# Two 1024-wide scans per unit, the carried state added by GpSimd, and a C product shared differently between VectorE and GpSimd

## The reference

```python
def step(h, inputs):
    u_t, dt_t, B_t, C_t = inputs
    dA = jnp.exp(dt_t[:, :, None] * A[None])
    dBu = (dt_t * u_t)[:, :, None] * B_t[:, None, :]
    h = dA * h + dBu
    y = jnp.einsum('bdn,bn->bd', h, C_t)
    return (h, y)
...
A = -jnp.exp(A_log)
y = _selective_scan(u_c, dt, A, Bm, Cm, D)
y = y * jax.nn.silu(z)
out = jnp.einsum('ble,de->bld', y, W_out)
return x + out
```

## Time and profile before

| | |
|---|---|
| time, median of 3 runs | 2322.84 us (2321.6 to 2324.49) |
| time of the profiled execution | 2327.84 us |
| its span, first to last instruction | 2325.9 us |
| busy: TensorE / VectorE / ScalarE / GpSimd | 77% / 81% / 78% / 83% |
| mean granted clock of TensorE | 0.888 of full speed |

### The profile page before, as it was taken

How to read it: one execution, slowest core, us unless ns; L and a number is a source line. 1 busy time by engine, 2 the same in 40 slices (tenths; PEclk the granted TensorE clock), 3 DMA queues, 4 the chain that set the end, 5 groups by cost and what they waited for, 6 DMA issues and landing times.

```text
span 2325.9 us, 32531 instructions
## 1 busy us (share of the span) xinstructions
PE 1795.3 (77%) x7694; PEld 923.0 (40%) x7694; DVE 1893.7 (81%) x2437; ACT 1806.5 (78%) x3753; POOL 1933.7 (83%) x1190
## 2 busy tenths in 40 slices
PE   5566768697878788797878788797878788666785
PEld 2112323153534344353434444353434344343542
DVE  0389988899889888899889888899889888999221
ACT  5888888888898788888998788888998787763332
POOL 1588897989999898999999898999999898987333
PEclk9888978797989898998989898997989898786998
DMA  1635454477777786677777786677777786797332
GB/s 57 145 83 141 105 141 109 125 177 184 169 178 178 169 213 160 170 183 184 174 175 180 163 218 157 171 183 180 176 179 178 160 221 147 183 259 221 70 49 34
DMA packets 217979, 369.34 MB, mean 159 GB/s; under 512 B 31040, under 2 KB 86592, under 8 KB 217664
## 3 DMA queue, kind: packets, MB, share of 16 engines
q1 hardware_dynamic: 192208, 333.56, 58.1%
q0 software_dynamic: 25584, 33.71, 7.5%
HBM read 285.05 MB, written 83.01 MB: 158 GB/s over the span
## 4 chain that ended last, share of the span: by engine, by line
issue 23%; POOL 23%; ACT 18%; PE 18%; DVE 9%; DMA 8%; POOLq 0%; ACTq 0%; DVEq 0%; SPq 0%
DMA out<-yt,xt 8%; POOL arena L1324 8%; DVE dA L1116 5%; PE ring L603 5%; ACT dA L979 4%; POOL arena L1332 4%; POOL out L1372 3%; POOL sorted_x L1362 2%; PE yps L697 2%; PE ring L611 2%; DVE arena L1116 2%; POOL arena L1347 2%; POOL arena L1342 1%; PE p_g L729 1%; PE ring L640 1%
## 5 line engine op out<-in xcount | busy, mean ns | idle before, releaser
L1324 POOL TENSOR_TENSOR arena<-arena,b_bc 128x2048 f32<-128x2048 f32 x256 | 998.4, 3900 | 88.3 <-PE yps L697 88.3
L979 ACT ACTIVATE dA<-arena,a_s 128x512 f32<-128x512 f32 x1024 | 680.5, 684 | 116.0 <-DVE arena L1125 69.9
L1116 DVE TENSOR_TENSOR_SCAN dA<-dA,arena 128x512 f32<-128x512 f32 x384 | 454.5, 1213 | 156.8 <-ACT dA L979 107.3
L1116 DVE TENSOR_TENSOR_SCAN dA<-dA,carry,arena 128x512 f32<-128x512 f32 x384 | 477.6, 1274 | 52.3 <-POOL arena L1324 36.2
L697 PE MATMUL yps<-arena,const_s 128*32 128x512 f32 x2048 | 320.4, 702 | 59.9 <-POOL arena L1332 35.9
L1332 POOL TENSOR_TENSOR arena<-arena,c_bc 128x511 f32<-128x511 f32 (+1 forms) x256 | 335.0, 1308 | 28.3 <-DVE arena L1116 26.5
L1125 DVE TENSOR_TENSOR arena<-dA,c_bc 128x1024 f32<-128x1024 f32 x256 | 313.6, 1225 | 8.8
L1372 POOL DMA_INDIRECT out<-yt,xt x135 | 215.0, 1592 | 115.7 <-ACT yt L1020 84.1
L595 PE MATMUL ring<-arena 128*128 128x512 f32 x488 | 265.4, 670 | 55.5 <-ACT arena L883 21.6
L729 PEld LDWEIGHTS p_g<-xT,w_e 128*128 128x128 f32 x1680 | 216.7, 209 | 127.5 <-issue 127.5
L603 PE MATMUL ring<-arena 128*128 128x512 f32 x480 | 236.8, 639 | 35.3 <-ACT arena L883 13.6
(11 more groups left out here) (171 smaller groups left out, 2973.5 us busy)
## 6 DMA issues: line engine op xcount, KB each, us to landing
arena<-dt_d SPq DMA_DIRECT2D x512, 256.0 KB
w_e<-in_w_moe SPq DMA_DIRECT2D x105, 512.0 KB, 4.7
dt_d<-arena SPq DMA_DIRECT2D x128, 256.0 KB, 2.4
w_e<-in_w_moe SPq DMA_DIRECT2D x105, 256.0 KB
xt<-sorted_x SPq DMA_DIRECT2D x135, 129.0 KB
b_bc<-bc_d SPq DMA_DIRECT2D x256, 64.0 KB, 2.4
c_bc<-bc_d SPq DMA_DIRECT2D x256, 64.0 KB, 5.3
xs<-in_x SPq DMA_DIRECT2D x16, 512.0 KB, 4.4
```

Source lines behind the costliest of these rows:

```text
L979: act.activation(dA[:, j, :], rep_dt[:, c % 2, j, :], ACT.Exp, scale=a_s[:, n, j:j + 1]).then_inc(s_exp, 1)
L1116: return dve.tensor_tensor_scan(out_ap, dA[:, j, :], hs[:, u % 3, j, :], init, ALU.mult, ALU.add)
L1324: pool.tensor_tensor(hs[:, u % 3], rep_dtu[:, c % 2], b_bc[:, g, :].unsqueeze(1).to_broadcast([P, J, T]), ALU.mult).then_inc(s_dbu, 1)
```

## The change

1. The four 512-wide scans of a unit become two of 1024, over segments 0 and 1 and over 2 and 3. So that the state doesn't run from one segment into the next, the first decay of each segment has to be 0: column 0 of rep_dt is set once to 1e30 (NEVER) and the loads skip it, so that the exponential of a negative rate times it gives 0.
2. With the decay at 0, the carried state of an odd block can no longer come in as an initial value. It is multiplied by the true first decay and added to the driving term's column 0. For this the first two columns of dt are loaded apart (`load_first`, into dt0), `first_rates` (GpSimd) multiplies them by the rates, `first_decay` (ScalarE) takes the exponential, `first_carry` (GpSimd) multiplies the carries of 4 units, and `add_carry` (GpSimd) adds them, 128 x 4, before the unit's scans.
3. The product with C of segments 2 and 3 is done as one of 128 x 1024: by GpSimd (`weigh`) in the 8 units of POOLED, whose scan writes to hs, and by VectorE (`unit_last`) in the other 8. GpSimd's `weigh` moves to the end of its slot.
4. `keep2` and `keep3` become one `keep23` ahead of the decay of segment 2, and the decay of segment 3 moves behind that of segment 2. TensorE no longer waits for `keep3`'s product.
5. The rates are negated by VectorE, and bounded from zero by 1e-26 (SLOWEST).

```diff
+POOLED = (0, 4, 5, 6, 7, 9, 12, 15)
+
+
+def pooled(u):
+
+    return u % UN in POOLED
...
+                    skip = 1 if k == 0 else 0
                     for r in part:
-                        sp.dma_start(dst[32 * r:32 * r + 32, c % 2], src).then_inc(s[c % 2], 16)
+                        sp.dma_start(dst[32 * r:32 * r + 32, c % 2, :, skip:], src[:, :, skip:]).then_inc(s[c % 2], 16)
+
+            def load_first(q, c):
+
+                sp.wait_ge(s_dtw[c % 2], 32 * (2 * q + c // 2 + 1))
+                wait(sp, s_first, CC * (q // 2) + c - 1)
+                src = dt_d[q % 2, 0, c].rearrange("(j d) t -> d j t", j=J)
+                for r in range(R):
+                    sp.dma_start(dt0[32 * r:32 * r + 32, c % 2], src[:, :, 0:2]).then_inc(s_dt0[c % 2], 16)
...
+                if 0 <= q < NQ and q % 2 == 1 and n in (0, 4, 8):
+                    load_first(q, n // G + 1)
+                if q >= 0 and front and q % 2 == 0 and n == 12:
+                    load_first(q + 1, 0)
...
             def weigh(u):
                 q, n = u // UN, u % UN
                 c, g = n // G, n % G
-                if q % 2 == 0:
-                    pe.wait_ge(s_last, UN * (q // 2) + n + 1)
                 if g == 0:
                     wait(pe, s_yg, CC * q + c)
                     pe.matmul(yps[:], d_skip[:, c, :], uc[:, q % 2, c, :], start=True, stop=False, skip_group_check=True)
-                pe.wait_ge(s_m2, u + 1)
-                pe.wait_ge(s_hp, u + 1)
+                pe.wait_ge(s_m01, u + 1)
+                if pooled(u):
+                    pe.wait_ge(s_hp, pooled_to(u))
+                else:
+                    pe.wait_ge(s_m23, kept_to(u))
...
-                wait(act, s_m01 if j < 2 else s_m2 if j == 2 else s_h3, u)
-                if u > 0 and (u - 1) // UN % 2 == 0 and j != 3:
-                    act.wait_ge(s_carry01 if j < 2 else s_carry2, UN * ((u - 1) // UN // 2) + (u - 1) % UN + 1)
+                if u == 0:
+                    act.wait_ge(s_rate, 1)
+                if j < 2:
+                    wait(act, s_m01, u)
+                elif u > 0 and pooled(u - 1):
+                    act.wait_ge(s_h23, pooled_to(u - 1))
+                elif u > 0:
+                    act.wait_ge(s_m23, kept_to(u - 1))
+                if u > 0 and (u - 1) // UN % 2 == 0:
+                    act.wait_ge(s_carry01 if j < 2 else s_carry23, UN * ((u - 1) // UN // 2) + (u - 1) % UN + 1)
                 act.activation(dA[:, j, :], rep_dt[:, c % 2, j, :], ACT.Exp, scale=a_s[:, n, j:j + 1]).then_inc(s_exp, 1)
 
             def keep01(u):
                 act.wait_ge(s_m01, u + 1)
                 act.activation(carry[:, u % UN, 0:2], dA[:, 0:2, T - 1], ACT.Copy).then_inc(s_carry01, 1)
 
-            def keep2(u):
-                act.wait_ge(s_m2, u + 1)
-                act.activation(carry[:, u % UN, 2:3], dA[:, 2, T - 1:T], ACT.Copy).then_inc(s_carry2, 1)
-
-            def keep3(u):
-                q, n = u // UN, u % UN
-                count = UN * (q // 2) + n + 1
-                act.wait_ge(s_h3, u + 1)
-                act.activation(carry[:, n, 3:4], hs[:, u % 3, 3, T - 1:T], ACT.Copy).then_inc(s_carry3, 1)
-                act.wait_ge(s_carry3, count)
-                act.wait_ge(s_c[n % G], 64 * (q + 1))
-                act.activation(hs[:, u % 3, 3, T - 1:T], carry[:, n, 3:4], ACT.Copy, scale=c_bc[:, n % G, T - 1:T]).then_inc(s_last, 1)
+            def keep23(u):
+                if pooled(u):
+                    act.wait_ge(s_h23, pooled_to(u))
+                    ends = hs[:, u % 3, 2:4, T - 1]
+                else:
+                    act.wait_ge(s_m23, kept_to(u))
+                    ends = dA[:, 2:4, T - 1]
+                act.activation(carry[:, u % UN, 2:4], ends, ACT.Copy).then_inc(s_carry23, 1)
+
+            def first_decay(q, c):
+
+                act.wait_ge(s_first, CC * (q // 2) + c + 1)
+                act.activation(e0[:], e0[:], ACT.Exp).then_inc(s_e0, 1)
...
+                for p, c in firsts(s + 1):
+                    first_decay(p, c)
...
-                if 0 <= s + 1 < UN * NQ:
-                    decay(s + 1, 3)
                 for g, k in tiles_in(s - 3, False):
                     take_y(g, k)
                 for item in taken_in(s, 3):
                     take(item)
-                if 0 <= s < UN * NQ and q % 2 == 0:
-                    keep2(s)
                 for item in taken_in(s, 4):
                     take(item)
                 for g, k in tiles_in(s):
                     take_xt(g, k)
+                if 0 <= s < UN * NQ and q % 2 == 0:
+                    keep23(s)
                 if 0 <= s + 1 < UN * NQ:
                     decay(s + 1, 2)
-                if 0 <= s < UN * NQ and q % 2 == 0:
-                    keep3(s)
+                    decay(s + 1, 3)
...
-            def scan(u, j):
+            def rates():
+
+                dve.wait_ge(s_a, 1)
+                dve.tensor_scalar(a_s[:], a_s[:], -1.0, SLOWEST, ALU.mult, ALU.min).then_inc(s_rate, 1)
+
+            def scan(u, j, out):
+
                 q, n = u // UN, u % UN
-                first = q % 2 == 0
-                init = 0.0 if first else carry[:, n, j:j + 1]
-                out_ap = hs[:, u % 3, j, :] if j == 3 else dA[:, j, :]
-                dve.wait_ge(s_exp, J * u + (1, 2, 4, 3)[j])
+                dve.wait_ge(s_exp, J * u + j + 2)
                 dve.wait_ge(s_dbu, u + 1)
-                if not first:
-                    dve.wait_ge((s_carry01, s_carry01, s_carry2, s_carry3)[j], UN * (q // 2) + n + 1)
-                return dve.tensor_tensor_scan(out_ap, dA[:, j, :], hs[:, u % 3, j, :], init, ALU.mult, ALU.add)
-
-            def unit_first(u):
+                if q % 2 == 1:
+                    dve.wait_ge(s_inject, UN * (q // 2) + n + 1)
+                return dve.tensor_tensor_scan(out.rearrange("p j t -> p (j t)"), dA[:, j:j + 2].rearrange("p j t -> p (j t)"),
+                                              hs[:, u % 3, j:j + 2].rearrange("p j t -> p (j t)"), 0.0, ALU.mult, ALU.add)
+
+            def weigh(u, j):
                 q, n = u // UN, u % UN
                 g = n % G
-                scan(u, 0)
-                scan(u, 1).then_inc(s_scan, 1)
-                dve.wait_ge(s_scan, 2 * u + 1)
                 dve.wait_ge(s_c[g], 64 * (q + 1))
-                dve.tensor_tensor(hs[:, u % 3, 0:2], dA[:, 0:2], c_bc[:, g, :].unsqueeze(1).to_broadcast([P, 2, T]),
-                                  ALU.mult).then_inc(s_m01, 1)
-
-            def unit_third(u):
-                scan(u, 3).then_inc(s_h3, 1)
+                return dve.tensor_tensor(hs[:, u % 3, j:j + 2], dA[:, j:j + 2], c_bc[:, g, :].unsqueeze(1).to_broadcast([P, 2, T]), ALU.mult)
+
+            def unit_first(u):
+                scan(u, 0, dA[:, 0:2]).then_inc(s_scan, 1)
+                dve.wait_ge(s_scan, kept_to(u) + pooled_to(u) + kept_to(u - 1))
+                weigh(u, 0).then_inc(s_m01, 1)
 
             def unit_second(u):
-                scan(u, 2).then_inc(s_scan, 1)
+                if pooled(u):
+                    scan(u, 2, hs[:, u % 3, 2:4]).then_inc(s_h23, 1)
+                else:
+                    scan(u, 2, dA[:, 2:4]).then_inc(s_scan, 1)
 
             def unit_last(u):
-                q, n = u // UN, u % UN
-                g = n % G
-                dve.wait_ge(s_scan, 2 * u + 2)
-                dve.tensor_tensor(hs[:, u % 3, 2], dA[:, 2], c_bc[:, g, :], ALU.mult).then_inc(s_m2, 1)
+                dve.wait_ge(s_scan, u + 1 + kept_to(u))
+                weigh(u, 2).then_inc(s_m23, 1)
...
-                if unit:
-                    unit_third(s)
...
-                if unit:
+                if unit and not pooled(s):
                     unit_last(s)
...
+            pool.memset(rep_dt[:, :, :, 0], NEVER).then_inc(s_init, 1)
...
-                pool.wait_ge(s_h3, u + 1)
+                pool.wait_ge(s_h23, pooled_to(u))
+                if q % 2 == 0:
+                    pool.wait_ge(s_carry23, UN * (q // 2) + n + 1)
                 pool.wait_ge(s_c[g], 64 * (q + 1))
-                end = T - 1 if q % 2 == 0 else T
-                pool.tensor_tensor(hs[:, u % 3, 3, 0:end], hs[:, u % 3, 3, 0:end], c_bc[:, g, 0:end], ALU.mult).then_inc(s_hp, 1)
+                pool.tensor_tensor(hs[:, u % 3, 2:4], hs[:, u % 3, 2:4], c_bc[:, g, :].unsqueeze(1).to_broadcast([P, 2, T]),
+                                   ALU.mult).then_inc(s_hp, 1)
+
+            def add_carry(u):
+
+                q, n = u // UN, u % UN
+                pool.wait_ge(s_dbu, u + 1)
+                pool.wait_ge(s_w0, CC * (q // 2) + n // G + 1)
+                pool.tensor_tensor(hs[:, u % 3, :, 0], hs[:, u % 3, :, 0], carry[:, n, :], ALU.add).then_inc(s_inject, 1)
+
+            def first_rates(q, c):
+
+                pool.wait_ge(s_dt0[c % 2], 64 * (2 * (q // 2) + c // 2 + 1))
+                pool.wait_ge(s_rate, 1)
+                wait(pool, s_w0, CC * (q // 2) + c)
```

(20 more changed lines are left out.)

53 lines of the change are left out of this document (34 added, 19 removed).

## The result

The kernel after takes 2426.85 us (median of 4 runs, 2422.56 to 2427.84) against 2323.66 of the kernel before on the same chip: 1.0436 times, with an interval of 1.0414 to 1.0457. It is 103 us slower. The forecast of 2297 us had the wrong sign, and the time lies above the range and above every rival.

A forecast was written before the change was run, and what follows sets the result against it. It took GpSimd's queue to bound units 10 to 3 and a fixed chain units 4 to 9. Terms of -12, -9 and -5 made -26 us: 2301.8 from 2327.8, 2297 as median of runs; range 2260 to 2340.

The forecast's parts named there:

- The bound: Units 10 to 3: GpSimd binds, busy 77.6 of 80.2 us; units 4 to 9: a chain of fixed length sets the pace.
- VectorE: 1024-wide scans of 2.27 us and moved products save VectorE 3.4 us an even block, 7.6 an odd one.
- GpSimd, even block: 16 products of 512 at 1.04 us become 8 of 1024 at 1.96: GpSimd's work falls 1.0 us a block.
- GpSimd, odd block: Carry steps add 4.5 us (add_carry) and 2.0 (first_rates, first_carry); with the product's -1.0, work rises 5.5 us.
- Order and new waits: Units 4 to 9: new waits, including weigh's for keep23, bring drive(11) 2.3 us later in even blocks, 0.5 in odd.
- the +0.5: Odd blocks, units 4 to 9: drive(11) comes 0.5 us later than in the kernel before.
- The gain itself: Units 10 to 3, GpSimd-bound: lighter queue takes 4.5 us off an even block; carries leave -0.2 in an odd one.
- DMA cover: The 8-byte dt0 loads and 2044-byte rows leave two slots before they are needed, so they cost nothing.
- The sum: Even blocks -2.2 us, odd +0.3; blocks 4 to 14 -12, blocks 0 to 2 -9, block 15 -5: -26 us.
- terms outside blocks 4 to 14: Blocks 0 to 2 gain 2.5, 4 and 2.5 us, block 3 counts 0, block 15 gains 5; start and end untouched.
- GpSimd's waits stay: Rival, chance 0.13: GpSimd keeps its idle time in every block, so only its work counts: +36 us, 2359 us.
- GpSimd at its floor: Rival, chance 0.17: no waits beyond issue gaps; blocks take 123.8 us even, 129.3 odd, mean 126.7; 2266 us.

The follow-up runs named there:

- e_kept_4: Kernel before, with segment 3's product moved from GpSimd to VectorE, done together with segment 2's, in units 1, 10, 11 and 14: 2299.36 us, 0.9884.
- e_keep_kept: Kernel after without the carries' steps, and without keep23 and the waits for it in the 8 pooled units: 2329.81 us, 1.0024 of the kernel before.
- the first probe: Kernel before plus one VectorE 128x4 product a unit, both inputs in SBUF, between the scans and unit_first's product: 2658.17 us, 1.1428.

## Why the prediction was wrong

**The bound.** That GpSimd's queue decides, and not what VectorE saves, holds: it is 30% of the chain after, and taking work from GpSimd in e_kept_4 gains 26 us. But I treated the queue as an amount of work. The work grew by 22 us (forecast +36), and the time by 103.

**VectorE.** The scan takes 2294 ns (forecast 2270), the product 1224. Busy time should have fallen by 8 x 3.4 + 8 x 7.6 = 88 us; it fell by 5. But 61 us of the time after is small instructions that stand longer (means of the groups L1211, L1215, L1229 and L1231 after, 686 + 1270 + 1587 + 1420 ns, less 587 + 243 + 158 + 162 before, times 16), so its real work fell by 66. Right in kind, and worth 26 us where VectorE binds; it doesn't in the kernel after.

**GpSimd, even block.** 2.00 us a product, as forecast, and -0.2 us a block where -1.0 was forecast. The price was right. The ratio of the Trainium skill, "GPSIMD Engine Reference", section 3.1, which gave 2.4 us, stands against a mean of 2.09 us here, overlap counted: the trace doesn't agree with it.

**GpSimd, odd block.** `add_carry` takes 0.21 us: the work is +3.0 instead of 5.5. Here lies the first failed step: I counted the carries' steps as work alone, 6.5 us an odd block, of which 4.3 in the stretch that GpSimd binds. Their records add up to 5.0 (26.1 + 7.1 + 7.1 us over eight blocks), but GpSimd stands still around them: before `add_carry` (12.1 us in all), before `first_carry`, which waits for ScalarE's exponential (13.9), and before the indirect DMAs (26). That makes 6.5 us more an odd block, with no term in my sum, and the next drive, and VectorE's scan behind it, come later by it. Without the carries the odd blocks 5 to 13 are 9.0 us shorter, and the change costs 60 us instead of 103.

**Order and new waits.** The step that failed worst. I had named the wait of GpSimd's `weigh` for keep23 in units 6 and 7, of 3.5 us, and then priced what reaches the path at 2.3 us in an even block. In unit 6 it came as forecast (3.4 us from the scan's end to the product in block 8, of which GpSimd was idle 2.4). But GpSimd stands 92.7 us for this copy, 11.6 an even block, and seven tenths of it in units that I had not looked at: 4, 5, 9, 15, 0 and 12 (unit 15 is the one shown above, with three steps of ScalarE ahead of the copy). Removing it gives 54 us back without carries, and 24 with them. I followed drive(11) alone; in other units also the product is what the next drive stands behind. In odd blocks, where there is no copy to wait for, the product's own wait is 17 us in all and most of the loss is the carries'; the +0.5 left that out.

**The gain itself.** The sum took 4.5 us off units 10 to 3 for GpSimd's lighter queue. With carries and that wait both gone (e_keep_kept) these units of blocks 4 to 13 last 78.6 us in the mean against 80.2, here block 7:

```profile
1071.04:1149.27 78.23, 59.17 (x287) 32.51 (x286) 70.70 (x52) 67.91 (x128) 73.92 (x43) 0.96 0.71 177
```

GpSimd's work fell by 3.7 us there in the mean, and the time by 1.6. Units 4 to 9 took 1.2 us longer. So even without both causes the change was worth less than a microsecond a block.

**The moved `weights` and `place`.** I had no term for it, and this is the third step that failed: `unit_third` was removed ahead of them, and I costed only what moves and not what stays and thereby falls into another engine's time. Moving them back behind a scan gives 18 to 21 us, but 7 once keep23's wait is gone and the carries stay.

**DMA cover.** Costed at nothing, rightly: `first_rates` (L1402) shows 0.0 us of idle before it, so the 8-byte loads are in time.

**The sum.** By one way of taking the change apart the steps are: 1024-wide scans with carries 30, place of the small steps 21, copies of state 53 less the 23 that before pays too, and 21 for the rest of the split; 30 + 21 + 30 + 21 = 102. It adds up because each is the difference of two neighbouring runs, not because the effects are independent: along the other way the carries are 42.5 and keep23's wait 54. Open is what makes up the last 21 us (the place of `weigh` at the end of the slot, or `unit_last`'s 1024-wide product in front of ScalarE's decays), how much of the whole goes by the clock, and why `weights` and `place` at the unit's end, without pooled units, costs 34 us. Not tried was `weigh` in its old place in the slot with the rest of the change.

**The rivals.** "GpSimd's waits stay" had the right sign and engine, and its time of 2359 was too low since it let idle time stay where it grew, from 8 to 13 us a block to 14 to 20. The odd blocks were forecast to be longer than the even ones by up to 5 us, and are by 4.6 in the mean. "GpSimd at its floor" has a slip: with 6.5 us of carries on 123.8 its odd block is 130.3, not 129.3; its mean of 126.7 is that of 130.3, so its time stands. None of the terms outside blocks 4 to 14 came either: blocks 0 to 2 are together 7.5 us longer instead of 9 shorter, block 15 is 3.4 longer instead of 5 shorter.

## What to carry to other kernels

For a step put on an in-order queue, write down who waits for it and what it waits for, in every unit, before counting its microseconds. The 0.2 us of `add_carry` held a scan 0.3 us more and the indirect DMA behind it 0.45 us more, and the 0.2 us of a copy held a product and the 3.8 us drive queued behind it; each cost tens of us. When a product moves between engines, keep the state's copy out of its way (leave out the column that is copied). And look at what a removed instruction used to separate: a neighbour of it can slide into another engine's transfer. The gain here was in a small step of the same change, units whose product goes to VectorE, without new waits.

## What the runs showed of the hardware

A VectorE instruction of 128x4 with both inputs in SBUF takes 0.16 us when GpSimd has no tensor instruction in work (27 of the 256 in the first probe, 161 to 164 ns) and up to 4.96 us when it has (214 of the other 229 over 0.2 us); it takes 0.162 us (at most 0.164, 256 times) in the same place with one input in PSUM. The big C products, which read dA in PSUM, never showed it (1224 ns in the mean and 1228 at most, as before). The Trainium skill says this in "SBUF — State Buffer", section "SBUF: two separate sides": VectorE and GpSimd share a pair of ports, and a VectorE operation with two SBUF inputs and a GpSimd one that reads SBUF exclude each other for a whole instruction. The trace agrees, and shows besides that the waiting instruction got no turn between two GpSimd instructions that follow each other (1404.55 to 1409.5). It also shows a TENSOR_SCALAR with one SBUF input standing (L1229, 1587 ns in the mean against 158 before).

An indirect DMA of GpSimd for which the profile names no other wait starts 0.15 us after a 128x2048 product and 0.6 us after a 128x4 add (medians of 48 and 42 in the kernel after, those that write `out`). Which of the two differences makes it, the size or the add, no run shows.
